# Reordering the start of a gated feed-forward kernel: the first gate emptied ahead of two weight sums, tiles 2 to 5 made one by one

## The reference

```python
def _L0_xattn_ref(x, adj, W, b):
    si = jnp.einsum('bnd,d->bn', x, Wi[0])
    sj = jnp.einsum('bnd,d->bn', x, Wj[0])
    xij = jax.nn.sigmoid(si[:, :, None] + sj[:, None, :] + b[0])
    return P_ASEM * xij + (1.0 - P_ASEM) * adj

def _L0_ffn_ref(x, w1, w2, w3):
    # _bitlinear: RMS norm, rows quantised to 8 bits, weights to -1, 0, 1
    gate = jax.nn.silu(_bitlinear(x, w1))
    up = _bitlinear(x, w2)
    return _bitlinear(gate * up, w3)
x = x + jnp.tanh(g_xattn[0]) * _L0_xattn_ref(ctx_512, _layernorm(x, axis=-1), L0_xattn_W, L0_xattn_b)
x = x + jnp.tanh(g_ffn[0]) * _L0_ffn_ref(_layernorm(x, axis=-1), L0_ffn_w1, L0_ffn_w2, L0_ffn_w3)
```

## Time and profile before

| | us |
|---|---|
| median of three executions (lowest, highest) | 157.48 (156.69, 157.88) |
| the profiled execution | 155.58 |
| its span, from the first instruction to the last | 153.8 |
| PE busy | 137.7 (90%) |
| DVE busy | 119.3 (78%) |
| ACT busy | 106.7 (69%) |
| POOL busy | 96.8 (63%) |

### The profile page before, as it was taken

How to read it: one execution, slowest core, us unless ns; L and a number is a source line. 1 busy time by engine, 2 the same in 40 slices (tenths; PEclk the granted TensorE clock), 3 DMA queues, 4 the chain that set the end, 5 groups by cost and what they waited for, 6 DMA issues and landing times.

```text
span 153.8 us, 2452 instructions
## 1 busy us (share of the span) xinstructions
PE 137.7 (90%) x754; PEld 76.4 (50%) x754; DVE 119.3 (78%) x185; ACT 106.7 (69%) x174; POOL 96.8 (63%) x151
## 2 busy tenths in 40 slices
...
DMA packets 45381, 26.94 MB, mean 175 GB/s; under 512 B 35767, under 2 KB 38072, under 8 KB 45368
## 3 DMA queue, kind: packets, MB, share of 16 engines
...
...
## 4 chain that ended last, share of the span: by engine, by line
PE 67%; POOL 12%; DMA 7%; DVE 6%; issue 3%; SPq 2%; ACT 2%; ACTq 0%; DVEq 0%; POOLq 0%
PE ps L1255 42%; PE ps L1299 23%; DMA c_all<-in_x_dram 7%; POOL raw L502 2%; POOL ln_r L433 2%; POOL w3q L505 2%; PE ps L1294 2%; DVE raw_room L980 1%; SPq L287 1%; POOL xq L487 1%; POOL c_all L448 1%; ACT raw_room L704 1%; POOL slope_mean L437 1%; DVE w1T L985 1%; POOL slope L436 1%
## 5 line engine op out<-in xcount | busy, mean ns | idle before, releaser
L1255 PE MATMUL ps<-w1T,xqT 128*128 128x512 f16 (+1 forms) x192 | 40.6, 361 | 0.1
L1255 PE MATMUL ps<-w2T,xqT 128*128 128x512 f16 (+1 forms) x192 | 40.7, 361 | 0.0
L1004 DVE SCALAR_TENSOR_TENSOR raw<-ps,deq,raw_room 128x1408 f32<-128x1408 f32 x16 | 26.9, 1684 | 16.2 <-PE ps L1255 8.4
L1299 PE MATMUL ps<-w3T,hqT 128*128 128x512 f16 x165 | 37.7, 379 | 0.0
L704 ACT ACTIVATE raw_room<-ps,deq 128x1408 f32<-128x1408 f32 x16 | 22.9, 1430 | 12.3 <-PE ps L1255 12.3
L514 POOL TENSOR_SCALAR hq<-raw,h_scale 128x1408 f16<-128x1408 f32 x15 | 22.1, 1473 | 12.1 <-DVE h_scale L1014 11.7
L1255 PEld LDWEIGHTS ps<-w2T,xqT 128*128 128x128 f16 x192 | 18.7, 98 | 19.9 <-DVE raw L1004 0.6
L1255 PEld LDWEIGHTS ps<-w1T,xqT 128*128 128x128 f16 x192 | 18.6, 98 | 19.7 <-ACT raw_room L704 0.4
L715 ACT ACTIVATE junk<-raw 128x1410 f16<-128x1410 f32 x16 | 21.9, 1371 | 7.6 <-DVE raw L1004 7.6
L1011 DVE TENSOR_REDUCE h_top<-raw 128x1 f32<-128x1409 f32 x16 | 25.8, 1610 | 0.2
L1299 PEld LDWEIGHTS ps<-w3T,hqT 128*128 128x128 f16 x165 | 16.0, 98 | 18.2 <-issue 0.3
...
## 6 DMA issues: line engine op xcount, KB each, us to landing
c_all<-in_x_dram SPq DMA_DIRECT2D x16, 256.0 KB, 9.4
out_dram<-out_ring SPq DMA_DIRECT2D x15, 256.0 KB, 2.3
...
hq<-in_ctx_dram SPq DMA_DIRECT2D x4, 256.0 KB, 10.2
...
```

Source lines behind the costliest of these rows:

```text
L1004: v.scalar_tensor_tensor(out=hid[:, t % HS, 0:H], in0=ps_up[:, 0:H], scalar=deq[:, 1, t:t + 1], in1=gate[:, t % GATES, :], op0=ALU.mult, o ...
L1255: last = m.matmul(bank[:, lo:hi], xqT[:, i % XT, k, :], wT[w][:, k, lo:hi], start=(k == 0), stop=(k == KD - 1))
L1299: last = m.matmul(ps_y[t % 2], hqT[:, t % HT, k, :], w3T[:, :, k, :], start=(k == 0), stop=(k == KH - 1))
```

## The change

Four things change; no arithmetic does, and no transfer is added or removed.

1. **PE, ACT:** on ACT `ctx_out(2)` and `silu(0)` go ahead of the last two sums of |w3|. On PE `scores(2)`, `turn_w(1, 4)` and `gate_product(1)` go ahead of `sum_w(2)`; `gate_product(2)` goes ahead of `turn_ctx(3)`, and `up_product(1)` ahead of `scores(3)`.
2. **Parts:** `make_x`, `max_x` and what waits for them count in `PARTS`, in which tiles 2, 3, 4 and 5 are single. `step_x`, `dequant_x` and `intercept` keep their pairs.
3. **Intercepts:** one `scalar_tensor_tensor` for a unit in the place of a `tensor_scalar` for each tile.
4. **Order of tiles 2 to 5:** on POOL, DVE, ACT and SP the calls between `mean_x(0)` and tile 6 are put in another order. On ACT `silu(1)`, `silu(2)` and `silu(3)` go to earlier places. `turn_h(0)` and `turn_x(5)` go ahead of `turn_w3(2)`.

```diff
+    PARTS = [(0, 1), (1, 2), (2, 3), (3, 4), (4, 5), (5, 6)] + UNITS[4:]
+    PART = [n for n, (lo, hi) in enumerate(PARTS) for _ in range(lo, hi)]
...
             turn_x(4)
+            turn_h(0)
+            turn_x(5)
             turn_w3(2)
-            turn_x(5)
-            turn_h(0)
             turn_w3(3)
...
             def quant_x(i):
-                pool.wait_ge(x_scaled, UNIT[i] + 1)
+                pool.wait_ge(x_scaled, PART[i] + 1)
...
             mean_x(0)
+            quant_x(2)
             conv_w(2, 0)
-            quant_x(2)
             quant_x(3)
+            step_x(2)
+            dequant_x(2)
+            slopes_x(3)
             conv_w(2, 1)
-            slopes_x(3)
-            step_x(2)
             conv_w(2, 2)
-            dequant_x(2)
             quant_x(4)
             quant_h(0)
+            conv_w(2, 3)
+            quant_x(5)
             step_x(3)
-            quant_x(5)
+            dequant_x(3)
             mean_x(1)
-            dequant_x(3)
-            conv_w(2, 3)
...
-                for i in range(lo, hi):
-                    ins = v.tensor_scalar(icept[:, i:i + 1], th_sum[:, i:i + 1], t03_neg[:, 0:1], slope_mean[:, i:i + 1],
-                                          ALU.mult, ALU.subtract)
-                ins.then_inc(icepts, 1)
+                v.scalar_tensor_tensor(out=icept[:, lo:hi], in0=th_sum[:, lo:hi], scalar=t03_neg[:, 0:1],
+                                       in1=slope_mean[:, lo:hi], op0=ALU.mult, op1=ALU.subtract).then_inc(icepts, 1)
...
-            def make_x(u):
-                lo, hi = UNITS[u]
+            def make_x(n):
+                lo, hi = PARTS[n]
...
-            scale_w(2)
+            half_scores(2)
             make_x(2)
             max_x(2)
-            half_scores(2)
+            make_x(3)
+            scale_w(2)
+            max_x(3)
             stats_x(3)
             stats_x(4)
+            hidden(0)
             clip_w3(0)
-            hidden(0)
-            clip_w3(1)
             intercept(3)
             max_h(0)
+            clip_w3(1)
+            make_x(4)
             half_scores(3)
-            make_x(3)
-            max_x(3)
+            max_x(4)
             hidden(1)
-            weight_factor(2)
+            make_x(5)
+            max_x(5)
             clip_w3(2)
             intercept(4)
-            max_h(1)
             hidden(2)
             clip_w3(3)
-            make_x(4)
-            max_x(4)
+            weight_factor(2)
+            max_h(1)
+            make_x(6)
+            max_x(6)
             hidden(3)
```

More of the change, by code:

```diff
@@ L673, in score @@
                 if i >= 4:
[L674 removed]
+                    act.wait_ge(made, PART[i - 4] + 1)
                 if i // TB in DIRECT:
@@ L685, in square_x @@
             def square_x(i):
-                act.wait_ge(made, UNIT[i] + 1)
+                act.wait_ge(made, PART[i] + 1)
                 if i >= 2:
@@ L791, in _ @@
             scores_out(3)
-            silu(3)
             affine_x(6)
@@ L1117, in _ @@
             stats_x(7)
-            make_x(5)
-            max_x(5)
+            make_x(7)
+            max_x(7)
             intercept(6)
@@ L1126, in _ @@
             affine_x(11)
-            make_x(6)
+            make_x(8)
             max_h(7)
-            max_x(6)
+            max_x(8)
             add_x(3)
@@ L1135, in _ @@
             hidden(9)
-            make_x(7)
+            make_x(9)
             intercept(8)
```

50 lines of the change are left out of this document (25 added, 25 removed).

## The result

| | us |
|---|---|
| changed kernel, median of four executions (lowest, highest) | 157.87 (157.22, 159.89) |
| kernel before, four executions beside them | 157.08 (154.81, 157.88) |
| changed over before | 1.0176, 95% interval 1.0122 to 1.0229 |
| profiled execution of the changed kernel, its span | 157.41, 155.6 |

The change makes the kernel slower, by 1.8% or some 2.7 us; the forecast was 0.6%. The time itself, 157.87, lies inside the forecast's range of 156.5 to 159.2; the loss against the kernel before is three times the one forecast. The ratio leaves out executions more than 1.5% above the fastest of their kernel.

A forecast was written before the change was run, and what follows sets the result against it. PE was taken to bound the kernel, through the start of gate_product(5). Waits gone -1.81, tile 2's wait and uncovered pieces +1.8, ACT chain +0.9 took the profiled 155.58 to 156.5, on the median 158.4; range 156.5 to 159.2.

The forecast's parts named there:

- The bound: PE sets the time from 47.87 to the last store; only the start of gate_product(5), 57.52 before, counts.
- Part 1: Sum of |w3| behind gate_product(1): PE's waits of 1.41 and 0.40 go, up_product(0) could start 1.81 earlier.
- Part 2: Transposed tile 2 for gate_product(2): issued 1.5 earlier, held by the loads' backlog, landing at 41.4; PE idles about 2 us.
- part 3: Moved pieces between the products, to gate_product(3): PE even with before; the new intercept costs at most the two it replaces.
- the sum: Shift of gate_product(5): -1.81 for waits gone, +1.8 for tile 2 and uncovered pieces, +0.9 for the ACT chain.
- h tile 1: Its transpose, read by last_product(1), might come late behind tile 6 on POOL: estimated nothing to 0.3, taken as nothing.
- Part 4: Order on ACT: silu(3) ahead of five more pieces, silu(4) starts at 57.0, gate_product(5) at 58.45, 0.9 later.
- the 0.93: Delay of gate_product(5) from ACT's chain, 58.45 against 57.52 before, stated as 0.9 later.
- Rival D: The transpose issued into the loads' tail slows it; tile 2 lands at 42.0, gate_product(5) 1.5 late; 159.2, chance 0.15.

The follow-up runs named there:

- e12: e10 with the loads of tiles 10 to 15 of x again ahead of the transposes of tiles 2 and 3; median 157.80.
- e10: e5 with scale_w(2) ahead of make_x(3), max_h(0) ahead of intercept(3) and quant_h(1) ahead of quant_x(6); median 157.00.
- e1: The changed kernel with the old intercepts, one tensor_scalar for each tile; median 157.24, ratio to the kernel before 1.0041.
- e3: The changed kernel with the loads of tiles 10 to 15 of x issued behind the transposes of tiles 2 and 3; median 158.17.
- e5: The changed kernel with old intercepts and the loads of tiles 10 to 15 behind the first transposes; median 156.79, ratio to before 1.0119.
- e11: e10 with the new intercepts, one scalar_tensor_tensor for a unit; median 157.88.
- e15: e5 with scale_w(2) ahead of make_x(3), clip_w3(1) behind hidden(1), slopes of tiles 4 to 7 halved, dependent calls reordered; 157.61, ratio to before 1.0165.
- e4: e1 with silu(3) back in its old place on ACT, behind the five pieces; median 158.09, 157.25 at full clock.
- e2: The kernel before with the new intercepts alone; median 159.21, ratio to before 1.0174, no execution at full clock.
- e7: The kernel before with part 1 of the change alone, the pairs kept; median 155.65, ratio to before 1.0024.
- e6: The kernel before with the loads of tiles 10 to 15 behind the transposes of tiles 2 and 3; median 157.84, none at full clock.
- e14: The kernel before with row maxima of h of tiles 0, 1 and 2 over the last 176 columns only; 155.91, ratio to before 0.9998.
- e17: e15 with w3's transposes issued earlier, max_h(3), max_h(4) and quant_h(4) moved ahead; median 155.80, ratio to before 0.9987.

## Why the prediction was wrong

- **What was right.** The bound: PE from `gate_product(5)` on, with nothing given back. In starts from `gate_product(0)` the forecast had `gate_product(2)` at 41.45 - 28.78 = 12.67 (measured 12.78), `gate_product(3)` at 18.68 (18.78), the wait for tile 2 at about 2 us (1.99), idle ACT ahead of `silu(3)` of about 1 (0.89), a single `make_x` at 0.75 (0.74). Part 1's 1.81 came (`up_product(0)` starts 1.75 earlier) and went as foreseen.
- **Part 2 was right by luck.** Its issue came 0.5, not 1.5 us earlier in this count, since `intercept(2)` held DVE 0.8 longer and `make_x(3)` held `quant_x(2)` to 1.11; its landing took 3.0, under the 4 forecast. Two misses that cancel. In the time of the trace the issue is at 37.51 (forecast 37.35) and the landing at 40.5 (forecast 41.4); no engine moves anything from 40.0 to 41.0, so the tail was through before the 40.3 of the forecast. That the tail of the loads lengthens the transpose is shown by e12 against e10 (4.0 and 2.4) and e1 (4.7). It isn't what made the kernel slower, by e3 and e5.
- **The step that failed: part 3, "it costs between nothing and the two it replaces, and sits on no path here".** It takes up to 1.31 against 0.46, and it sits on the path of DVE to `hidden(1)`, and of ACT to `silu(4)` over `affine_x`. By e10 and e11 its price is 0.9 us, by e3 and e5 some 1.35, which is half or more of the 1.8 us by which the sum below was short. Most of the rest is h tile 1, the term taken as nothing. The earlier trace rows held hints, and so did two rows of POOL before, of the same instruction: 1.14 beside DVE's pair of 35.05 to 36.38, and 0.20 alone.

```profile
35.30 1.14 POOL L478 TENSOR_TENSOR deq<-x_step,w_deq 128x2 f32<-128x2 f32 x1
```

```profile
45.93 0.20 POOL L478 TENSOR_TENSOR deq<-x_step,w_deq 128x4 f32<-128x4 f32 x1
```

- **Left out: hidden(1).** Part 3 followed DVE to `hidden(0)` and stopped; the sum then let `up_product(2)` start at 50.28 - 28.78 = 21.50. It started at 22.64, 1.1 later, with its wait of 0.89. What holds `hidden(1)` is DVE's chain, and its waits for POOL: after, 0.80 idle and then 1.31 for `intercept(3)`. In e15 `up_product(2)` came at 20.05 with `stats_x(4)` and `clip_w3(1)` moved away.
- **Part 4, mis-sized.** `silu(4)` forecast at 28.2, measured at 28.8: its chain is 7.41 in the place of 6.9, by the 0.50 that `affine_x(6)` waits for the intercept. So `gate_product(5)` is 1.55 late, not 0.93. Whether the 0.93 itself is due to `silu(3)` going first, as the forecast has it, stays open: e4 did not get it back, but its tile 2 came 1.4 later than after. In e5, with old intercepts and an early tile, `gate_product(5)` is still 0.81 late, and there PE waits for `hidden(1)` (1.11) and tile 4 (0.39), not for ACT.
- **"For h tile 1 I take nothing": it cost 0.66**, and 0.13 came ahead of it. It is POOL's order: POOL stands idle 5.18 ahead of `quant_x(6)`, with `quant_h(1)` behind it. In e10, with `quant_h(1)` first, that stretch is as short as before; the next product then waits 0.25 for DVE. Another 0.36 came between `up_product(5)` and `up_product(12)`, in the changed kernel and not in e1 (49.9, as before): again the new intercepts, since `up_product(12)` waits for DVE in e2, e3 and e11 too, and in no kernel with the old ones. 0.62 (gate_product(5)) + 0.79 + 0.36 is the 1.8 us by which the sum was short.
- **Rival D**, slower by over 1%, had the sign, but not the mechanism: it took the loss from a late tile 2, and tile 2 was not late (12.78 against 12.80 before).

## What to carry to other kernels

Look at the operands before you put one instruction in the place of two. Here the one was shorter than the pair (0.20 against 0.45) only where POOL was in nothing long; with its second tensor from SBUF it otherwise lasted until POOL was through, 1.3 us for 0.2 us of work. Price a move by following every engine to the product behind the one it helps, not only to the first that would wait. Where five engines are each just in time, an earlier product shows the next thing that was just in time; the orders tried here moved the wait from a weight sum to a row tile, to a block of w3 and to h, and kept nothing at full clock.

## What the runs showed of the chip

**Clock.** The granted clock falls to about half, the 1.2 GHz level, for a few microseconds in some executions; I call that a spell. In the trace after it is at 22 to 26, ahead of the start from which I count (the last column but two is the clock, a mean of 0.57):

```profile
22.00:26.00 4.00, 3.56 (x28) 3.17 (x29) 3.86 (x11) 3.57 (x8) 3.11 (x4) 0.57 1.05 409
```

In e7's trace it comes behind 1.98 us of idle PE, and the product then takes 4.22 in the place of 2.54:

```profile
41.44 4.22 PE L1255 MATMUL ps<-w1T,xqT 128*128 128x512 f16 x12 [1.98 <-DMA xqT<-xq]
```

Counted by a mean clock below 0.998: the orders that wait for the sum ahead of `gate_product(1)` (before, e2, e6, e14) have such spells in 82 of 121 executions, those with part 1 and the loads ahead (the changed kernel, e1, e4, e7, e12) in 16 of 38, those with part 1 and the loads behind in 6 of 78. The kernel before on e17's chip had medians of 155.49 without one, 157.53 at a mean clock of 0.987 to 0.989 (three executions) and 158.98 at 0.978 (four). That is some 1.5 to 2 us for each step down, but no rule: two more at 0.966 and 0.967 took 157.84 and 157.30, and on other chips single executions with a spell are as short as those without (154.82 on e7's chip). One execution of the kernel before had a mean clock of 0.60 and took 246.38. That idle PE around 30 to 41 us brings a spell on is what the counts speak for, but they don't show it: e7 waits 1.98 for tile 2 and has one spell in ten executions, and e6, whose PE waits only 0.73 for the sum, has spells in all four. What starts a single spell stays open.

**Transposes in a tail of loads.** A transpose of 128 x 512 takes 2.3 alone. Tile 2 takes 2.4 or 2.5 in all kernels with six loads behind it. With all loads ahead it takes 2.6 in the kernel before and in e2, 3.0 after, 3.3 in e7, 3.4 in e14, 4.0 in e12, 4.7 in e1 and 4.9 in e4. An earlier issue can land later: e1's comes 0.3 earlier than after's and lands 1.4 later. The kernel before and e14, with the same calls until there, differ by 0.8, so a single trace doesn't say which change of order made a landing longer.
